# Second halves of the turn back and of the bias of a chunk, one expert step later, behind that step's second layer

## What is computed

```python
h = jnp.einsum('bfd,edh->bfeh', x, W1) + b1
h = jax.nn.relu(_bn(h, g1, be1, m1, v1))
h = jnp.einsum('bfeh,ehk->bfek', h, W2) + b2
h = jax.nn.relu(_bn(h, g2, be2, m2, v2))
y = jnp.einsum('bfeh,ehd->bfed', h, Wo) + bo
return jnp.einsum('bfed,fe->bfd', y, w)
```

## Time and profile before

| | us |
|---|---|
| median of 3 runs | 3103.85 |
| lowest and highest run | 3103.13, 3107.77 |
| profiled execution, its own time | 3106.59 |
| its span, first to last instruction | 3104.8 |
| TensorE busy, VectorE busy, ScalarE busy, GpSimd busy | 2828.3, 2183.9, 1972.1, 1516.6 |

### The profile page before, as it was taken

How to read it: one execution, slowest core, us unless ns; L and a number is a source line. 1 busy time by engine, 2 the same in 40 slices (tenths; PEclk the granted TensorE clock), 3 DMA queues, 4 the chain that set the end, 5 groups by cost and what they waited for, 6 DMA issues and landing times. The chain is left out here.

```text
span 3104.8 us, 41557 instructions
## 1 busy us (share of the span) xinstructions
PE 2828.3 (91%) x15504; PEld 2380.5 (77%) x15504; DVE 2183.9 (70%) x4084; ACT 1972.1 (64%) x2738; POOL 1516.6 (49%) x1530
## 2 busy tenths in 40 slices
PE   5689899999999999998999998788899999999998
PEld 5567777777777777777777777677788898988988
DVE  7688787878878777877878784498555555555544
ACT  6467676777767767676776775325455555655554
POOL 1577777777777777777777777631000000000000
PEclk9899999999999999999999999899899999999999
DMA  7567676767767666666666666410424333243231
GB/s 221 168 231 245 232 249 232 248 233 241 242 228 248 216 213 225 214 220 218 220 219 215 219 214 226 150 44 24 139 102 138 130 107 122 101 137 114 102 109 58
DMA packets 164927, 559.97 MB, mean 180 GB/s; under 512 B 31190, under 2 KB 68374, under 8 KB 157556
## 3 DMA queue, kind: packets, MB, share of 16 engines
q1 hardware_dynamic: 87492, 355.23, 31.0%
q0 software_dynamic: 77232, 202.08, 22.7%
HBM read 320.19 MB, written 237.00 MB: 179 GB/s over the span
## 5 line engine op out<-in xcount | busy, mean ns | idle before, releaser
L647 POOL DMA_INDIRECT ring<-runs,src_i x1436 | 1431.1, 997 | 509.3 <-issue 380.4
L980 PE MATMUL ps<-oh,zhl 128*128 128x512 f32 x3136 | 1287.7, 411 | 131.6 <-DVE oh L819 130.3
L982 PE MATMUL ps<-oh,zhl 128*128 128x512 f32 x3136 | 1258.6, 401 | 0.0
L813 DVE SCALAR_TENSOR_TENSOR ring<-ring,pen 128x256 f32<-128x256 f32 x1564 | 750.7, 480 | 379.2 <-DMA ring<-runs,src_i 363.1
L669 ACT ACTIVATE oh<-ids,nodeneg 128x512 fp32r<-128x512 f32 x896 | 639.8, 719 | 481.2 <-PE ps L982 480.9
L980 PEld LDWEIGHTS ps<-oh,zhl 128*128 128x128 f32 x3136 | 610.9, 195 | 289.7 <-DVE oh L819 166.2
L982 PEld LDWEIGHTS ps<-oh,zhl 128*128 128x128 f32 x3136 | 610.6, 195 | 121.7
L674 ACT ACTIVATE oh<-oh,ones 128x512 fp32r<-128x512 f32 x896 | 613.3, 708 | 0.0
L819 DVE TENSOR_SCALAR oh<-ps,nodef 128x512 fp32r<-128x512 f32 x672 | 501.0, 746 | 3.3 <-PE ps L982 2.8
L1512 ACT ACTIVATE av<-ps,vecs 128x896 f32<-128x896 f32 x224 | 246.3, 1100 | 348.6 <-PE ps L191 348.6
L1627 DVE TENSOR_TENSOR h2l<-av,h2h 128x896 fp32r<-128x896 f32 x112 | 122.3, 1092 | 212.6 <-ACT h2h L1514 212.6
(11 more groups left out here) (279 smaller groups left out, 3645.7 us busy)
## 6 DMA issues: line engine op xcount, KB each, us to landing
runs<-ring SPq DMA_DIRECT2D x136, 896.0 KB, 4.2
fw<-wsp SPq DMA_DIRECT2D x56, 1536.0 KB, 6.5
runs<-ring SPq DMA_DIRECT2D x102, 768.0 KB
ring<-runs,src_i POOLq DMA_INDIRECT x1436, 2.8
ids<-srcT_d SPq DMA_DIRECT2D x32, 256.0 KB, 5.3
res_d<-x_all SPq DMA_DIRECT2D x7, 896.0 KB
y<-res_d SPq DMA_DIRECT2D x7, 896.0 KB, 7.5
part<-in_Wx SPq DMA_DIRECT2D x16, 384.0 KB, 7.1
```

Source lines behind the costliest of these rows:

```text
L647: pool.indirect_dma_start(ring[:, k, :], None, runs[0:N, :], bass.IndirectOffsetOnAxis(ap=src_i[:, STEPS * i + k:STEPS * i + k + 1], axis= ...
L813: dve.scalar_tensor_tensor(out=ring[:, k, :], in0=ring[:, before, :], scalar=pen[:, STEPS * i + k:STEPS * i + k + 1], in1=ring[:, k, :], o ...
L980: pe.matmul(ps[:, two + k, :], z_hi(g)[:, v, cols], oh[:, v, :], start=g == 0 and v == 0, stop=False, skip_group_check=True)
L982: r = pe.matmul(ps[:, two + k, :], z_lo(g)[:, v, cols], oh[:, v, :], start=False, stop=False, skip_group_check=True)
```

## The change

Four places change. On TensorE, turn_v(c + 1, 1) leaves the end of e = 0 (behind L3) and stands in e = 1 between L2 and L1; bias(c, 1) leaves the end of e = 2 and stands in e = 3 between L2 and L1. On VectorE, x_one(c + 1, 1) leaves the end of e = 0 and bias_in(c, 1) the end of e = 2; they stand in e = 1 and e = 3 behind the low parts of h2 and ahead of the low part of h1's first block. No instruction, wait, buffer or DMA is added or removed.

```diff
--- before.py
+++ after.py
@@ -1666,6 +1666,10 @@
                         low(2 * n + 1, m, h2h, h2l)
                     if n == 0:
                         softmax(0)
+                    if e == 1 and c < LAST:
+                        x_one(c + 1, 1)
+                    if e == 3:
+                        bias_in(c, 1)
                     if more:
                         low(2 * n + 2, 0, h1h, h1l)
                     weighted(n, 0)
@@ -1684,15 +1688,11 @@
                     weighted(n, 2)
                     weighted(n, 3)
                     if e == 0:
-                        if c < LAST:
-                            x_one(c + 1, 1)
                         stack_lo(c)
                     if n == 0:
                         dve.wait_ge(s_bos, 1)
                         dve.tensor_tensor(bos[SLOT:SLOT + NE, :], bo[SLOT:SLOT + NE, :], bos[SLOT:SLOT + NE, :].bitcast(F32),
                                           ALU.subtract).then_inc(s_bol, 1)
-                    if e == 2:
-                        bias_in(c, 1)
                     if c < LAST:
                         if e == 1:
                             measure(c + 1)
@@ -1819,6 +1819,10 @@
                     L2(n)
                     if n == 0:
                         turn_l(0)
+                    if e == 1 and c < LAST:
+                        turn_v(c + 1, 1)
+                    if e == 3:
+                        bias(c, 1)
                     if n + 1 < STEPN:
                         L1(n + 1)
                     if c < LAST:
@@ -1835,10 +1839,6 @@
                     if e == 2:
                         bias(c, 0)
                     L3(n)
-                    if e == 0 and c < LAST:
-                        turn_v(c + 1, 1)
-                    if e == 2:
-                        bias(c, 1)
 
 
 VECS = [("b1", 2), ("g1", 2), ("bt1", 2), ("bg", 4), ("gg", 4), ("btg", 4), ("b2", 2), ("g2", 2), ("bt2", 2),
```

## The result

The changed kernel takes 3092.08 us (median of 6 runs, 3088.88 to 3094.22), against 3105.33 us before (6 runs, 3103.13 to 3110.25). The ratio is 0.9958, with a 95% interval of 0.9948 to 0.9968: 13 us less, between 10 and 16. The profiled execution took 3088.88 us with a span of 3087.1.

What follows compares the result with a forecast made beforehand. The expert stage was taken as bound by TensorE's own queue, so only its waits or costlier matmuls move the end. Gains of 6.5 + 8.9 = 15.4 us took 3103.85 to 3088.4 us, range 3086.5 to 3094.5.

Steps and rivals of the forecast that it cites:

- The waits go and nothing takes their place: Expert stage, TensorE: waits ending e = 0 (6 times) and e = 2 (7 times) vanish, leaving 0.12 us before layer two.
- Part one: Second half of the turn, moved from e = 0 to e = 1: net 1.08 us a chunk, times 6, 6.5 us.
- Part two: Second half of the bias, moved from e = 2 to e = 3: net 1.27 us a chunk, times 7, 8.9 us.
- What is late next: Layer three to layer two: h1's second-block low part, behind weighted(n, 1), is the limit; freed places become like other steps.
- The 0.08 in each step: Start of layer two, untouched steps: it already waits some 0.08 us for the low part of h1's second block.
- VectorE's room: VectorE in e = 1 and e = 3: moved adds, needing 0.95 and 1.14 us, fit in its idle windows.
- Rival (a): Moved adds hold VectorE up to 2.05 us beyond their rows; 6 us given back, 3094.4 us; chance 0.05.
- Rival (c): TensorE's clock falls in the denser expert stage; a mean of 0.96 costs about 36 us, giving 3124; chance 0.02.
- The sum: Whole kernel: turn's 6.5 plus bias's 8.9 is 15.4 us less, from a median of 3103.85 to 3088.4 us.

## Why the prediction was right

**The waits go and nothing takes their place.** Right, at all 13 places: no idle time before lines 1717 and 1768, 0.12 us from layer three to layer two. The steps forecast at 15.7, 16.3, 15.3 to 15.4 and 15.2 to 15.3 are 15.73, 16.30, 15.34 and 15.22, and all others are unchanged within 0.01.

**Part one.** 1.08 a chunk, measured 1.07; 6.5 us, measured alone 6.44. The block of six behind layer two costs the 0.57 of turn_n's six, and layer one behind it is 0.10 longer where I took 0.09.

**Part two.** 1.27 a chunk, measured 1.30; 8.9 us, measured alone 9.15. The three matmuls take 2253.00 - 2252.65 = 0.35, as taken; layer one behind them takes 2257.89 - 2253.00 = 4.89, only 0.02 longer than 4.87, where I took 0.05. The small surplus is that: transposes make the next layer longer, the bias matmuls hardly do.

**What is late next.** Right, and shown by the two kernels that move or relieve the low part of h1's second block. The 0.08 in each step was a wait (0.07).

**VectorE's room.** Right that the adds fit. Rival (a) took 2.4 in e = 1 and 1.2 in e = 3 as what is left behind the add; measured 2.93 and 1.48. The step that was short: the prediction named layer two and the third and fourth parts of layer three as those that could be late, but added up VectorE's two waits alone. The third part is the one, and it had 0.24 us of slack of its own; the rest of the difference is small, in e = 1 mostly the overlap of VectorE's rows. The extra 2.05 of rival (a) would have cost about 0.6 in e = 3, not 0.85. Nothing of it happened: the add of line 1622 starts at 2256.20 and the low part behind it waits for ScalarE, not for VectorE.

**The clock.** Rival (c) did not happen; from the first to the last layer two the stage is at 1.00 and denser than before. "Granted 1.00 throughout" was read too widely from a rounded mean, though: the very last layer three ran at a mean of 0.74 before and at 0.76 after, which is about the same cost in both. Where the clock fell in this stage, in these runs, it fell behind a stand of TensorE, never in denser work (below).

**The sum.** 15.4 us, in the stage 15.59. The median fell by 13.25 us to 3092.08, 3.7 above the 3088.4 that I gave. Two things make this up: the median of the kernel before is 3105.33 with three more runs instead of 3103.85 (1.5 us), and the difference of the medians is 2.15 us under the forecast, and 2.3 under what the stage gained, within its interval of 10 to 16. The range had room for this since it was made wider upwards, for the spread of the runs. The steps bear the 15.4 out; that the median came out 3.7 us off and still inside is owed to that width.

## What to carry to other kernels

When two halves share one buffer, the second half wants a long piece of its own engine's other work between it and the reader of the first half, and another one between it and the next user: a later step alone gives nothing (33.30 us for the pair of steps, against 33.10 before and 32.03 in the changed kernel). Place the reader where its engine idles anyway, behind what others wait for, and compute the room up to the first consumer that it holds up, and from start to start. Where whole times scatter by more than the gain, the repeated steps of one profiled execution show what the medians of 10 to 35 runs on these chips could not: the intervals of their whole times are 12 to 23 us wide.

## What the runs showed of the hardware

TensorE's clock can fall behind a short stand, and doesn't always. With four more instructions on VectorE, TensorE stands idle for 1.91 us in the middle of layer three, in each of the seven e = 3. In five it goes on at the same pace (e = 3 takes 17.38). In two the clock falls behind the stand to the lower level of 1.2 GHz; this is chunk 1, TensorE's timeline and two windows (columns as above):

```profile
2896.38 0.28 PE L1818 MATMUL ps<-fw,h2h 128*128 128x256 f32 x1
2898.56 0.58 PE L1816 MATMUL ps<-fw,h2h 128*128 128x256 f32 x1 [1.91 <-DVE y L1634]
```

```profile
2883.45:2896.50 13.05, 13.05 (x77) 11.97 (x75) 9.07 (x11) 8.75 (x9) 0.00 (x0) 1.00 0.33 121
...
2898.50:2902.30 3.80, 3.74 (x18) 3.74 (x19) 2.55 (x6) 0.00 (x0) 0.00 (x0) 0.55 0.02 4
```

The step takes 18.86 us, 1.48 more than its five sisters, so this stand cost 2.16 + 1.48 = 3.6 us. In chunk 0 the surplus is 0.81 in e = 3 and 0.72 in e = 4. The stands of 1.04 us with three more, of 1.14 with the transposes behind layer one, and of 0.95 and 1.13 in the kernel before left the steps at their length in every place, and the clock at 1.00.

One longer stand is in every kernel: ahead of the very last layer three, which has no layer one in front of it, TensorE stands 3.35 us for the last low part of h2. Behind it the clock was lower in 12 of the 13 traced kernels, and that layer took 6.3 to 7.6 us; in one, that with four more, it stayed at 1.00 and took 5.02, from the first matmul's start to the last one's. These are the kernel before, the changed kernel, and the one with four more:

```profile
3091.96:3098.45 6.49, 6.49 (x41) 6.49 (x42) 2.15 (x5) 0.00 (x0) 0.00 (x0) 0.74 0.03 10
```

```profile
3074.48:3080.80 6.32, 6.31 (x41) 6.32 (x42) 2.14 (x5) 0.00 (x0) 0.00 (x0) 0.76 0.00 0
```

```profile
3599.90:3605.20 5.30, 5.13 (x42) 5.10 (x42) 2.37 (x7) 0.00 (x0) 0.00 (x0) 1.00 0.02 6
```

So 1.3 to 2.6 us are lost at the end of most of these kernels, and this part of the whole time varies without any change to it. The Trainium skill ("TensorE: Matmul & The Clock Gate", Part 1) says that the throttled state is the default and that activity releases it. The direction agrees: in this stage the clock fell behind stands alone and came back under work (1.00 again from 2902.30 us on in chunk 1). Why equal stands ended differently (2 of 7, and 12 of 13) is not shown by these runs.

Not settled: why the stages ahead of the expert stage take 500 us longer on the chips of the experiments. Over the same stretch, 45 to 1850 us, their TensorE is granted 0.88 to 0.89 instead of 0.96, and the DMA moves 184 to 186 GB/s instead of 226; which of the two is the cause, if either, was not tried.
